# Transposes of two attention units issued together on TensorE

## What is computed

```
h = layernorm(x) * (1 + ca) + sa
qkv = h @ weight_qkv.T          # 4 key/value groups, 4 query heads each, D = 128
attn = softmax(causal(q @ k.T / sqrt(128))) ; out = attn @ v
x = x + ga * (out @ weight_proj.T)
h = layernorm(x) * (1 + cb) + sb
x = x + gb * ffn(h)             # Hadamard-rotated gate/up (1024 wide), silu, down
```

## Time and profile before

| | us |
|---|---|
| median of 3 runs | 927.78 |
| lowest, highest | 926.73, 928.13 |
| profiled execution, its own time | 926.08 |
| span of the profiled execution | 924.3 |
| PE busy | 909.6 |
| DVE busy | 628.5 |
| ACT busy | 514.9 |
| POOL busy | 488.1 |

### The profile page before, as it was taken

The page is one execution under the profiler, slowest core; times in us unless marked ns, Lnnn a source line. Parts: engine busy times, 40 slices in busy tenths (PEclk is TensorE's granted clock), DMA queues, the critical chain, the costliest instruction groups (busy, mean ns, idle before and its releaser), DMA issues.

```text
span 924.3 us, 15010 instructions
## 1 busy us (share of the span) xinstructions
PE 909.6 (98%) x5480; PEld 804.3 (87%) x5480; DVE 628.5 (68%) x1297; ACT 514.9 (56%) x1121; POOL 488.1 (53%) x699
## 2 busy tenths in 40 slices
PE   6999999999999999999999999999999999999997
PEld 5889889888888898888888898888888998888886
DVE  6578668856786678647875787378757876764554
ACT  4376566745765566557664766476647667531111
POOL 1386638561866286708671867076717989410000
PEclk9999999999999999999999999999999999999999
DMA  8000100000001000000010000000001001000000
GB/s 284 1 24 1 40 1 24 1 29 1 24 1 40 1 23 1 29 1 23 2 41 1 24 1 29 2 1 24 1 1 69 1 14 62 1 23 0 23 23 23
DMA packets 10180, 21.21 MB, mean 23 GB/s; under 512 B 1280, under 2 KB 5760, under 8 KB 9984
## 3 DMA queue, kind: packets, MB, share of 16 engines
q1 hardware_dynamic: 9392, 20.11, 6.4%
q10 hardware_dynamic: 720, 0.21, 0.1%
HBM read 18.22 MB, written 2.10 MB: 22 GB/s over the span
## 4 chain that ended last, share of the span: by engine, by line
PE 94%; DVE 2%; ACT 2%; issue 1%; DMA 0%; SPq 0%; DVEq 0%; ACTq 0%
PE ps L1286 13%; PE ps L1129 13%; PE ps L1130 13%; PE ps L1131 13%; PE ps L1307 7%; PE ps L1304 7%; PE ps L1305 7%; PE ps L1269 7%; PE ps L1275 6%; PE ps L1272 6%; ACT prob L780 1%; PE ps L1153 1%; DVE ps L1042 1%; PE ps L1140 1%; PE ps L1265 1%
## 5 line engine op out<-in xcount | busy, mean ns | idle before, releaser
L625 POOL TENSOR_TENSOR rinv<-rsum,mone 128x1 f32<-128x1 f32 x256 | 140.9, 550 | 230.5 <-ACT prob L780 229.9
L1046 DVE TENSOR_TENSOR pt_lo<-ps,pt_hi 128x512 fp32r<-128x512 f32 x288 | 198.1, 688 | 64.6 <-ACT pt_hi L804 61.3
L804 ACT ACTIVATE pt_hi<-ps 128x512 fp32r<-128x512 f32 x288 | 171.2, 597 | 116.5 <-PE ps L1286 114.2
L780 ACT ACTIVATE prob<-ps,nmax 128x256 f32<-128x256 f32 (+28 forms) x256 | 180.7, 706 | 82.9 <-DVE nmax L1042 81.1
L630 POOL TENSOR_SCALAR prob<-prob,rinv 128x256 f32<-128x256 f32 (+28 forms) x256 | 190.2, 743 | 38.8 <-POOL rinv L625 38.5
L1042 DVE CUSTOM_DVE_ANT_0 ps<-ps,mask_f 128x256 f32<-128x256 f32 (+28 forms) x256 | 183.1, 718 | 38.6 <-PE ps L1275 33.0
L1286 PE MATMUL ps<-ident,prob 128*128 128x128 f32 x1152 | 172.6, 273 | 1.0 <-POOL prob L630 0.8
L1286 PEld LDWEIGHTS ps<-ident,prob 128*128 128x128 f32 x1152 | 140.4, 141 | 20.9 <-DVE pt_lo L1046 3.4
L1304 PE MATMUL ps<-pt_hi,v_hi 128*128 128x512 f32 x288 | 134.3, 466 | 0.0
L1307 PE MATMUL ps<-pt_lo,v_hi 128*128 128x512 f32 x288 | 114.1, 396 | 0.0
L1305 PE MATMUL ps<-pt_hi,v_lo 128*128 128x512 f32 x288 | 113.5, 394 | 0.0
(11 more groups left out here) (179 smaller groups left out, 1814.1 us busy)
## 6 DMA issues: line engine op xcount, KB each, us to landing
w_raw<-in_wqkv SPq DMA_DIRECT2D x8, 640.0 KB, 4.1
wp_raw<-in_wproj SPq DMA_DIRECT2D x8, 512.0 KB, 3.5
out_y<-prob SPq DMA_DIRECT2D x8, 256.0 KB, 2.3
x<-in_x SPq DMA_DIRECT2D x3, 512.0 KB, 12.2
prob<-in_wug SPq DMA_DIRECT2D x3, 512.0 KB, 4.1
prob<-in_wmod SPq DMA_DIRECT2D x1, 1024.0 KB, 9.6
wv_raw<-in_wv SPq DMA_DIRECT2D x4, 256.0 KB, 4.6
raw_down<-in_wdn SPq DMA_DIRECT2D x1, 1024.0 KB, 4.8
```

Source lines behind the costliest of these rows:

```text
L780: a_.activation(row(i, h).rearrange("p (a n) -> p a n", a=nb), score_banks(i, h).rearrange("p (a n) -> p a n", a=nb)[:, :, 0:w], ACT.Exp, ...
L1046: v_.tensor_tensor(pt_lo[:, n % 3, :], ring(t, "T", n), pt_hi[:, n % 3, :].bitcast(F32), ALU.subtract).then_inc(ptl_done, 1)
```

## The change

A new function `together()` goes over the finished list. In each turn it takes the units in pairs (3,4), (5,6), ... (33,34), in the last turn only up to (25,26). The stretch from T(n-1) to V(n-2) is rewritten: both transposes first, then one other item if the stretch holds at least two others (a score block or a chunk in most cases), then V(n-3) and V(n-2), then the other items. Nothing is added to or taken from the list: the counts of instructions stay.

Since V(n-3) now stands behind T(n) on PE, the end of T(n) no longer tells that `pt_hi` buffer n % 3 is free. So ACT waits for V(n-3) before hi(n).

```diff
--- before.py
+++ after.py
@@ -154,7 +154,21 @@
     return out
 
 
-WALK = walk()
+def together(order):
+
+
+    for t in range(TURNS):
+        for n in range(4, NU if t + 1 < TURNS else LAST[WINDOWS[2][0]] + 1, 2):
+            first = order.index((t, "T", n - 1, 0))
+            stop = order.index((t, "V", n - 2, 0)) + 1
+            pair = [(t, "T", n - 1, 0), (t, "T", n, 0), (t, "V", n - 3, 0), (t, "V", n - 2, 0)]
+            rest = [item for item in order[first:stop] if item not in pair]
+            cut = 1 if len(rest) > 1 else 0
+            order[first:stop] = pair[:2] + rest[:cut] + pair[2:] + rest[cut:]
+    return order
+
+
+WALK = together(walk())
 
 
 
@@ -801,6 +815,8 @@
                     waiting.append((t, n, h))
                 if what == "T":
                     act.wait_ge(t_done, this(t_done, t, n + 1))
+                    if n > 2:
+                        act.wait_ge(pv_done, this(pv_done, t, n - 2))
                     a_.activation(pt_hi[:, n % 3, :], ring(t, "T", n), ACT.Copy).then_inc(pth_done, 1)
                     if n != NU - 1:
                         exps()
```

## The result

The changed kernel takes 987.1 us (median of 5 runs, 984.23 to 988.1), the kernel before in the same comparison 927.44 (926.73 to 928.13, 5 runs). The ratio is 1.064, 95% interval 1.0627 to 1.0652: slower by 6.4%. I had forecast 968 and a range of 946 to 983. The direction was right, the size was not, and the time lies above the range. The profiled execution took 984.23 against 926.08 before, so there are 58.1 us to account for where I had 41.6.

A forecast was written before the change was run, and what follows sets the result against it. PE, busy 98% of the span, was taken as the bound. Waits of 7.2 us a turn, less 0.5 of earlier waits and the 1.4 gain, net 5.3; 41.6 in all on 926.08 gave 968, range 946 to 983.

The forecast's parts named there:

- rival 3: The second transposes, or the block behind, cost PE the 0.09 again; nothing saved, waits stay: 979 us, chance 0.09.
- The gain: One step from transposes to fp32r matmuls goes in each of 124 pairs, 0.087 each: 10.8 us saved, 1.4 a turn.
- (B): At score block S(5,3): PE waits for ACT's exponential of S(5,1), late behind a DVE chain; PE stands 2.7 us a turn.
- LF: DVE's layer-norm statistics, a link in the chain of (B) between lo(10) and `o_lo`; taken as 1.78 us.
- (C): At transposes T16: their ring place is L's, so they wait for ACT's modulation; 1.5 us a turn.
- (A): At transposes T4 and T6: their banks need lo(2) and lo(4); waits of 0.5 and 0.9, together 1.4 us a turn.
- (D): At Y(1), the projection of tile 1: hi(16) waits for V13, delaying lo(16) and `o_lo`; 0.5 us a turn.
- (E): At V35, turns 0 to 6: waits for hi(35), behind the exponential of the next turn's S(7,3); 1.0 to 1.1 us.
- The new wait of hi for a value product: At (B), hi(10) waits for V7; said to cost nothing there, V7 being done at 1.7.
- rival 4: The clock falls to 1.2 GHz behind (B), costing 1.4 us a turn again: +11, 979 us; chance 0.08.
- Rival 1: Only (A) and (B) happen, the long chains (C) to (E) are absorbed: +20, 946 to 948 us; chance 0.18.

The follow-up runs named there:

- bench: Kernel before plus four stretches of extra transposes and value matmuls at its end, single, paired, and each alone; 991.3 us in one run, added work included.
- lf_late: Changed kernel with the next layer norm's statistics on DVE moved behind score block S(5,2); 967.97 us, ratio 1.0442.
- no_b: Changed kernel without the pairs (9,10) and (11,12); 968.94 us, ratio 1.0453.
- c_only: Changed kernel with the pairs (13,14) and (15,16) alone; 942.93 us, ratio 1.0175.
- a_only: Changed kernel with the pairs (3,4) and (5,6) alone; 936.95 us, ratio 1.0109.
- four: Changed kernel with four `pt_hi` and `pt_lo` buffers instead of three, so hi need not wait for V(n-3); 970.81 us, ratio 1.047.
- fill: Changed kernel with seven extra unused 512-column matmuls a turn ahead of S(5,3), where PE would stand; 979.66 us, ratio 1.0561.
- gb_moved: Changed kernel with the second gate's five DVE steps moved from the end of turn 1 to among the chunks of turn 2; 981.32 us, ratio 1.0581.
- harmless: Changed kernel with only the 8 pairs a turn where no cost was forecast, (7,8) and (19,20) to (31,32); 941.82 us, ratio 1.0154.
- chunks: Changed kernel with only the chunk-stage pairs (27,28) and (29,30); 926.17 us, ratio 0.9992.

## Why the prediction was right in its direction and wrong in its size

The row that shows the first slip lay in the window of the earlier trace rows, and rival 3 says wrongly that no such row exists. Timeline of PE in the kernel before:

```profile
332.63 1.03 PE L1286 MATMUL ps<-ident,prob 128*128 128x128 f32 x8
333.42 0.48 PE L1304 MATMUL ps<-pt_hi,v_hi 128*128 128x512 f32 x1
```

Eight transposes in a row without a wait take 333.42 - 332.63 = 0.79, and not 2 x 0.35 = 0.70. The terms of the sum, one by one:

- **The gain, -10.8: wrong, 0.** The step that failed is the first one, "a step from float32 transposes to the fp32r matmuls costs PE 0.09". I compared two distances behind different neighbours (0.32 and 0.23) and never added up a whole group. The eight transposes at 283.85 take 0.79, and bench settles it at 22.67 to 22.67. So do the eight at 332.63 in the kernel before, above. The Trainium skill's page "TensorE: Matmul & The Clock Gate", section "Back-to-back issue gap", gives a distance by columns alone, with no term for what stood before, and by it alone the gain was 0. The rows agree that there is no such term worth 0.09; the distance itself is 0.224 to 0.236 here for 512 columns (0.229 on average over bench's sixty), above the page's 216 ns. I set it aside for the trace, but what I set against it was a reading of the trace. This outcome was my rival 3, with its reason the wrong way round: the 0.09 isn't paid again, it was never paid. It moves the sum by 10.8.
- **(B), 2.7: mechanism right, size 2.1 in standing, 1.8 in shift.** The term mis-sized is LF, 1.24 instead of 1.78. Its price came from a row in which DVE's last step ran beside a scaling on POOL; turns 0 and 7 of the same trace had the step at 0.17 to 0.18. The due time of S(5,3) was a little off too: I took V9 out at 0.87, where my own price for it was 0.78. Measured from T9 (at 272.29), S(5,3) is due after 5.11 instead of 4.9 and starts after 7.18 instead of 7.6. lf_late and no_b show the mechanism, each by taking it away.
- **(C) 1.5: right place, 1.1.** T16 waits for the modulation in all eight turns. c_only shows 1.57 for it when nothing stands ahead, so the price was right for the place alone; (B) pays half a microsecond of it.
- **(A) 1.4: 1.17.** The banks of T4 and T6, as forecast; 1.05 alone in a_only. T8, which I counted at nothing, costs 1.22 when alone and 0.12 here.
- **(D) 0.5 and (E) 1.1: right, 0.56 and 1.22.** (E) appears at S(0,1) and then at V35.
- **The new wait of hi for a value product.** I gave it nothing at (B). four puts it at 0.18 there and 0.94 in a turn.
- **The clock: missed as a part of the sum.** It was rival 4, at 0.08. The four falls at (B) cost 1.5 to 1.6 each, 6.2 together, and the fifth about 1 by what the longer wait leaves unexplained (3.3 - (2.98 - 0.69)). I had noticed that PE hardly stood in mid-run before; a stand of 2 us eight times was the thing to price, not to leave to a rival. fill shows that it is the clock: the same order and S(5,3) no earlier, without the falls. The longer the wait, the surer the fall, over all the traces: the wait of 2.96 to 2.98 at the end of turn 1 had one in five of five, (B)'s 1.90 in 8 of 16 (the changed kernel and gb_moved), its 1.74 to 1.77 in four in 1 of 8, and no wait up to 1.4 had one.
- **The end of turn 1: missed.** I worked the places in turn 2 and multiplied. Turn 1 has the gate's steps ahead of the maximum that (E) waits for: 3.2 more there, about 1 of it clock. gb_moved shows it.
- **The first T0, 1.22 late: no cause in the change.** PE's list up to there is the same. Both kernels start at the lower clock, and it rose at 19.28 instead of 16.36; among the experiments the same stretch differs by 0.03 to 1.58. So the clock of the kernel before was not at its full speed over the whole span, as I had read off a mean of 1.0: its 512-column matmuls start 0.43 apart from 13.92 to 14.77 and 0.23 apart from 16.67 on.

The 16.5 us between 58.1 and 41.6 lie, by turn, as follows. Ordinary parts of turns 0 to 6: 2.4, with 0.6 more in turn 0 (the absent gain of 1.4 a turn, less what (A) to (C) fell short of their prices). Clock falls at (B) in turns 3, 5 and 6: 4.7. The end of turn 1 and unit 33 there: 3.6. The last turn: 8.5 instead of 4.5, of which some 1.6 is its fall and 1.2 stands between units 25 and 29. The start: 1.2. Rival 1, that the long chains would be absorbed, is refuted: each of (C), (D) and (E) stands in every turn that has it.

The 1.2 between units 25 and 29 is a place of its own, which I had not priced. The last turn has no chunks, and T27 stands unpaired right behind the pair (25,26). PE's timeline of the changed kernel there, T27 and the first matmul of Y(2):

```profile
817.65 0.66 PE L1302 MATMUL ps<-ident,prob 128*128 128x128 f32 x4 [0.30 <-DVE pt_lo L1062]
...
819.41 0.38 PE L1145 MATMUL ps<-wp_hi,o_hi 128*128 128x256 f32 x1 [0.39 <-DVE o_lo L1067]
```

T27 waits for its bank, as T4 and T6 do, and Y(2) for `o_lo`, as Y(1) does. harmless, which has the pair, has 1.2 there too; chunks, a_only and c_only, which don't, have nothing. No run takes this pair alone.

## What to carry to other kernels

When one kind of instruction seems to cost more behind another, time a whole period of both orders, from one start to the same start later, since a single distance can be moved between neighbours by how starts are recorded. Where engines take their work in the order of one list, putting two items together asks for the second one's buffer earlier, and that costs whatever slack wasn't there; price it place by place, but with the waits that stand ahead, which hide part of it. And a new stand of PE has a second price, the clock behind it, and every once-only step near a stretched chain needs its own look.

## What the runs showed of the hardware that I had not expected

- Float32 transposes of 128 x 128 take 0.109 us each in a row (8.65 for 80), and the matmul behind them is recorded 0.08 us early. Whole periods add up, single distances don't.
- The granted clock fell to 1.2 GHz behind a wait of PE of 1.9 us with eight transposes ahead of it, in four of eight turns, and came back 3.4 us later each time. At the wait of 3.0 us at the end of turn 1 it fell in all five kernels that have it, and in fill came back only after 6.8. Seven matmuls in the gap of 1.9 us kept it at 2.4 GHz in all eight turns. Behind lf_late's wait of 0.65, and in a_only and c_only with waits of up to 1.4, it never fell.
- A 128 x 2 step on DVE took 0.17 us by itself and 0.67 to 0.78 while POOL scaled a tile (0.71 in the kernel before, 0.78 in lf_late, 0.67 to 0.69 in no_b), ending together with it. The Trainium skill, page "SBUF — State Buffer", section "Who interferes with whom", says that DVE and GpSimd share one pair of ports, that `tensor_scalar` can take it, and that the loser is blocked for the whole instruction of the other; these rows agree, 258.43 against 258.40 for the two ends. No run varies it by itself.
